# A preactivated 3x3 convolution: the sum of x taken from plane C, and the mean subtracted from C in place

## The chip, the cores and the metric

The kernel runs on one core of one Trainium2 chip. The metric is the device time of one execution in microseconds (us), the median of several runs. In the text TensorE is PE, VectorE is DVE, ScalarE is ACT, GpSimd is POOL and SyncE is SP, as in the rows.

## What is computed

The input x has 32 images of 128 channels and 56 x 56 pixels in float32. Each image is normalized in 32 groups of 4 channels, convolved with a 3 x 3 kernel whose weights take only the values Wp, 0 and -Wn, and added to x.

```python
def _quantize(weight, Wp, Wn):
    max_val = jnp.max(jnp.abs(weight))
    w_norm = weight / safe_max                       # safe_max = max_val, or 1 where that is 0
    delta = 0.05 * jnp.max(jnp.abs(w_norm))
    tern = where(w_norm > delta, 1.0, where(w_norm < -delta, -1.0, 0.0))
    return where(tern > 0, Wp[0] * tern, where(tern < 0, Wn[0] * tern, tern))

def _gn(v):                                          # groups of 4 channels, all pixels
    return ((g - mean(g)) / jnp.sqrt(var(g) + 1e-5)).reshape(v.shape)

out = x + conv3x3(_gn(x), _quantize(weight, Wp, Wn)) + bias
```

## The kernel before

**The planes.** The 128 channels lie on the partitions. The kernel pairs the image rows and forms four planes of 28 x 56 from an image: C, the sum of an even row and the odd row below it (less two means); D, odd less even; A, an odd row less the odd row before it; B, an even row less the even row after it. The 3 x 3 convolution of the two rows of a pair then needs four products of three taps, C, D, A and B, in place of six: C and A go to the even output rows, D and B to the odd ones. Each plane is scaled by 256 over the standard deviation and split into two float16 parts: hi on ScalarE (`make_hi`, line 394) and lo, the rest, on VectorE (`make_lo`, line 617). TensorE multiplies both parts with the ternary weights (`multiply`, line 786), in 24 matmuls for a product, four banks of 6. `lo X(k)` here is lo of plane X of image k.

**The statistics.** ScalarE sums x (`sum_x`, line 400, one pass over 3136 columns). A matmul with a matrix of group means turns the sum into a mean, one column in PSUM (`sum_mean`, line 772); ScalarE reads it as the negative mean and twice that (`take_mean`, lines 425 and 426). A second pass on ScalarE sums the squares of x less the mean (`sum_squares`, line 440), a second column gives the variance (`sum_var`, line 777), and VectorE and ScalarE make the scale of it (`variance`, `root`, `first_rstd`, `newton_factor`, `scale_of_x`). VectorE forms C with two means added in the same instruction (`make_c`, line 571), D (577) and A (583); GpSimd forms B (331). Only the outer row of A and of B needs the mean by itself: two short ScalarE instructions (`edges`, lines 433 and 434), which must be done before hi A and hi B.

**The slots.** Every engine runs through the same sequence of slots, written by hand: `emit(prev, now, nxt, far)` lists what the engine does while image `now` is multiplied, for the image after it (`nxt`) and the one after that (`far`). Waits are on semaphores with counts; no scheduler moves anything. In a middle slot k, TensorE does C(k), the variance of k+1, D(k), A(k), the mean of k+2, B(k). ScalarE does hi A(k), hi B(k), the root of k+1, the copy of C(k) out of PSUM (which A(k) waits for), the sum of x of k+2, the copy of D(k) (which B(k) waits for), hi C(k+1), the mean of k+2, hi D(k+1), the squares of k+2, the edges of k+1. VectorE does lo D(k), the variance of k+1, lo A(k), C, D and A of k+1 with the small steps of the scale between them, lo B(k), lo C(k+1), and four instructions that write output rows from PSUM (line 632). GpSimd does plane B of k+1 once lo C(k+1) is done, beside these four. The start has slots of its own: `first_slot` (k = -1, no product), `second_slot` (k = 0) and, on two engines, `third_slot` (k = 1).

**Data in and out.** SP loads x in halves into four buffers and stores the output; GpSimd's queue adds x to the output rows by an accumulating DMA. A buffer of x is loaded again when all planes, edges and squares of its image are done.

**The weights.** Before the first product VectorE finds the largest weight of a channel (line 525), TensorE turns the column, and `ternary_weights` (lines 530 to 540) divides the weights by the maximum and compares them; TensorE then turns them (`turn_weights`, line 751, 18 matmuls for C and D and 6 for A and B), VectorE casts them to float16 (line 561).

## Time and profile before

| | us |
|---|---|
| median of 3 runs (561.44 to 563.65) | 561.8 |
| span of the profiled execution | 559.9 |
| PE busy | 530.8 (95%) |
| DVE busy | 540.4 (97%) |
| ACT busy | 508.4 (91%) |
| POOL busy | 159.9 (29%) |

The span goes from the first to the last instruction of the one profiled execution; the rest of its time lies around it. Busy times are unions over an engine's instructions, which overlap at their ends (a start that lies up to 0.1 us ahead of the end in the row before it is no error). In the chain of work that ended last, PE has 46%, DVE 30%, time in which the engine waited for nothing that the profile shows 19%, and ACT 2%. TensorE's granted clock was 0.996 of full speed on average.

### The profile page before, as it was taken

The page shows a single profiled execution, that of the slowest core. Times are in us where ns is not written, and L with a number is a line of the kernel's source. Part 1 is how long each engine was busy: PE and PEld are TensorE (multiplying, and loading weights), DVE is VectorE, ACT ScalarE, POOL GpSimd, SP SyncE. Part 2 cuts the span into 40 slices and gives each one's busy share as a digit, 9 for nine tenths or more (in the row PEclk, how much of TensorE's full clock was granted, in tenths as well). Part 3 has the DMA queues.
Part 4 walks back from the last instruction along what each step waited for, and adds up shares of the span by engine and source line. Part 5 has one row for each costly group of instructions (what it writes and reads, how often), then busy time and mean ns, then how long its engine had stood idle before and what let it go on. Part 6 is the DMA issues. An engine that isn't in the chain of part 4 may idle for free.

```text
span 559.9 us, 9357 instructions
## 1 busy us (share of the span) xinstructions
PE 530.8 (95%) x3233; PEld 319.8 (57%) x3233; DVE 540.4 (97%) x507; ACT 508.4 (91%) x485; POOL 159.9 (29%) x105
## 2 busy tenths in 40 slices
PE   1898999999999999999999999999999999999994
PEld 0554565565656556555655655565565556556552
DVE  4998999999999999999999999999999999999995
ACT  4899999999999999999999999999999999999850
POOL 2021333312333321233332133333213333212330
PEclk9999999999999999999999999999999999999998
DMA  8539899999999999999999999999999999997765
GB/s 284 217 116 236 251 293 290 289 262 270 323 274 323 302 275 284 289 292 295 312 300 262 288 300 291 294 302 301 286 296 274 293 311 309 278 275 184 174 174 235
DMA packets 27960, 152.63 MB, mean 273 GB/s; under 512 B 3488, under 2 KB 3488, under 8 KB 27936
## 3 DMA queue, kind: packets, MB, share of 16 engines
q1 hardware_dynamic: 18576, 102.77, 48.5%
...
q14 instruction: 12, 0.10, 0.1%
...
## 4 chain that ended last, share of the span: by engine, by line
PE 46%; DVE 30%; issue 19%; ACT 2%; DMA 1%; DVEq 1%; ACTq 0%
PE odd_rows L786 23%; PE even_rows L786 22%; DVE parts L617 15%; DVE y L632 9%; DVE plane L583 1%; DMA x<-in_x_dram 1%; DVE newton L606 1%; DVE norm_scale L612 1%; ACT junk L440 1%; DVEq L158 0%; DVE neg_var L595 0%; DVE rstd L601 0%; PE odd_rows L777 0%; ACT junk L408 0%; PE odd_rows L772 0%
## 5 line engine op out<-in xcount | busy, mean ns | idle before, releaser
L786 PE MATMUL odd_rows<-parts,w_lhsT 128*128 128x385 f16 (+1 forms) x1536 | 266.1, 330 | 3.4 <-DVE parts L617 3.1
L786 PE MATMUL even_rows<-parts,w_lhsT 128*128 128x385 f16 (+1 forms) x1536 | 265.6, 330 | 2.9 <-DVE parts L617 1.9
L617 DVE SCALAR_TENSOR_TENSOR parts<-plane,norm_scale,parts 128x1568 f16<-128x1568 f32 x127 | 233.8, 1844 | 1.8 <-ACT parts L394 1.8
L331 POOL TENSOR_TENSOR plane<-x 128x1512 f32<-128x1512 f32 x31 | 105.8, 3413 | 374.3 <-DVE parts L617 374.3
L786 PEld LDWEIGHTS even_rows<-parts,w_lhsT 128*128 128x128 f16 x1536 | 150.1, 98 | 108.3 <-DVE parts L617 2.6
L394 ACT ACTIVATE parts<-plane,norm_scale 128x1568 f16<-128x1568 f32 x127 | 199.8, 1596 | 9.7 <-ACT plane L434 5.2
L786 PEld LDWEIGHTS odd_rows<-parts,w_lhsT 128*128 128x128 f16 x1536 | 147.9, 99 | 102.7 <-DVE parts L617 4.4
L440 ACT ACTIVATE junk<-x,negmean 128x3136 f16<-128x3136 f32 x32 | 92.9, 2904 | 0.1
L400 ACT ACTIVATE junk<-x 128x3136 f16<-128x3136 f32 x31 | 87.0, 2806 | 0.0
L632 DVE SCALAR_TENSOR_TENSOR y<-even_rows,out_scale,d_sb 128x784 f32<-128x784 f32 x62 | 63.7, 1027 | 0.0
L632 DVE SCALAR_TENSOR_TENSOR y<-odd_rows,out_scale,c_sb 128x784 f32<-128x784 f32 x62 | 63.6, 1026 | 0.0
L571 DVE SCALAR_TENSOR_TENSOR plane<-x,neg2mean 128x1568 f32<-128x1568 f32 x32 | 58.7, 1834 | 0.0
L577 DVE TENSOR_TENSOR plane<-x 128x1568 f32<-128x1568 f32 x32 | 57.0, 1783 | 0.6 <-ACT junk L408 0.6
L385 ACT ACTIVATE d_sb<-odd_rows,bias_sb,out_scale 128x1568 f32<-128x1568 f32 x32 | 52.7, 1647 | 5.0 <-PE odd_rows L786 5.0
L583 DVE TENSOR_TENSOR plane<-x 128x1512 f32<-128x1512 f32 x32 | 55.3, 1727 | 0.0
L379 ACT ACTIVATE c_sb<-even_rows,bias_sb,out_scale 128x1568 f32<-128x1568 f32 x32 | 53.0, 1657 | 1.2 <-PE even_rows L786 0.8
L344 POOL DMA_DIRECT2D y<-in_x_dram x61 | 52.8, 873 | 4.5 <-issue 4.5
L425 ACT ACTIVATE neg2mean<-odd_rows 128x1 f32<-128x1 f32 x32 | 5.5, 171 | 15.0 <-PE odd_rows L772 13.9
L777 PEld LDWEIGHTS odd_rows<-sums,group_mean 128*128 128x128 f32 x64 | 11.6, 194 | 5.6 <-issue 3.5
L772 PEld LDWEIGHTS odd_rows<-sums,group_mean 128*128 128x128 f32 x62 | 10.9, 190 | 4.2 <-DVE parts L617 1.8
L777 PE MATMUL odd_rows<-sums,group_mean 128*128 128x1 f32 x64 | 9.2, 213 | 3.4 <-ACT junk L440 3.4
L433 ACT ACTIVATE plane<-x,negmean 128x56 f32<-128x56 f32 x32 | 10.6, 332 | 0.0
...
## 6 DMA issues: line engine op xcount, KB each, us to landing
...
wp_sb<-in_L_conv_Wp_dram ACTq DMA_DIRECT2D x1, 0.5 KB, 7.6
wn_sb<-in_L_conv_Wn_dram ACTq DMA_DIRECT2D x1, 0.5 KB, 8.0
bias_sb<-in_L_conv_bias_dram ACTq DMA_DIRECT2D x1, 0.5 KB, 7.7
```

The lines of the kernel that those rows point to most:

```text
L331: nc.gpsimd.tensor_tensor(plane[B][:, 0:PAIRS - 1, :], even[:, 0:PAIRS - 1, :], even[:, 1:, :], ALU.subtract).then_inc(plane_ready[B], 1)
L344: pool.dma_start(y, of, accum_op=ALU.add).then_inc(residual_added[img.buf][h], 16)
L379: nc.scalar.activation(c_sb[:], product_ps(EVEN), ACT.Identity, bias=(no_bias if p else bias_sb)[:, 0:1], scale=out_scale[:, p, 0:1]).then ...
L394: nc.scalar.activation(part(img, j, HI), plane[j][:], ACT.Copy, scale=norm_scale[:, b_slice(img)]).then_inc(hi_ready[j], 1)
L400: nc.scalar.activation(junk[:], x_sb[img.buf][:].rearrange("p h w -> p (h w)"), ACT.Copy, accum_out=sums[:, img.buf, 1:2]).then_inc(sum_re ...
L440: nc.scalar.activation(junk[:], x_sb[img.buf][:].rearrange("p h w -> p (h w)"), ACT.Square, bias=negmean[:, b_slice(img)], accum_out=sums[ ...
L571: nc.vector.scalar_tensor_tensor(plane[C][:], xs[:, 0:H:2, :], neg2mean[:, b_slice(img)], xs[:, 1:H:2, :], ALU.add, ALU.add).then_inc(plan ...
L577: nc.vector.tensor_tensor(plane[D][:], xs[:, 1:H:2, :], xs[:, 0:H:2, :], ALU.subtract).then_inc(plane_ready[D], 1)
L583: nc.vector.tensor_tensor(plane[A][:, 1:, :], odd[:, 1:, :], odd[:, 0:PAIRS - 1, :], ALU.subtract).then_inc(plane_ready[A], 1)
L617: nc.vector.scalar_tensor_tensor(part(img, j, LO), plane[j][:], norm_scale[:, b_slice(img)], part(img, j, HI), ALU.mult, ALU.subtract).the ...
L632: nc.vector.scalar_tensor_tensor(rows_of(y_sb[img.buf], h, odd), product_ps(odd, 2 * h, 2 * h + 2), out_scale[:, p, 0:1], other[:, 2 * h:2 ...
L786: ins = nc.tensor.matmul(product_ps(odd, b, b + 1)[:, 0, :, to:to + n], w_lhsT[:, prod, kw, :], part(img, prod, which)[:, b * BANK_ROWS:(b ...
```

## The change

- The pass that sums x on ScalarE (`sum_x`, and `sum_first_x` in halves for image 0) is gone. VectorE forms C without the mean, with a multiplication by 1.0 in the place of the column of means, and lets the same instruction write its sum as the sum of x (`make_c`; `make_first_c` in halves). C is formed for `far`, one slot earlier than before, so there are two buffers for it (`plane[C]` and `other_c`).
- ScalarE adds the two negative means to C in place (`centre`), behind the squares of the same image and ahead of the edges.
- The weights are compared with plus and minus 0.05 of their maximum, without being divided: ten instructions become six.
- In the first slots the order changes on four engines: GpSimd forms plane B of image 0 once the ternary weights are there (VectorE did, `make_first_b`); TensorE turns the weights of C and D ahead of the first variance, and forms the mean of image 1 behind the wait for lo D(0) and its variance ahead of the last bank of D(0); VectorE forms C(1) ahead of the weight casts for A and B, and D(1) and A(1) in slot 0; ScalarE copies C(0) behind hi B(0).

```diff
-    def difference_b(img):
+    def difference_b(img, first=False):
-        pool.wait_ge(lo_ready[C], img.count(plus=1))
+        if first:
+            pool.wait_ge(w_ternary, p + 1)
+        else:
+            pool.wait_ge(lo_ready[C], img.count(plus=1))
...
-        if now and nxt:
-            difference_b(nxt)
+        if nxt:
+            difference_b(nxt, first=not now)
...
-    def sum_x(img):
-        act.wait_ge(x_loaded[img.buf], img.turn * 32 + 32)
-        wait(act, sumsq_ready, img.count())
-        nc.scalar.activation(junk[:], x_sb[img.buf][:].rearrange("p h w -> p (h w)"), ACT.Copy,
-                             accum_out=sums[:, img.buf, 1:2]).then_inc(sum_ready, 1)
-    def sum_first_x(img):
-        act.wait_ge(half_x_loaded, 16 * (p + 1))
-        wait(act, sumsq_ready, img.count())
-        halves = [x_sb[img.buf][:, 2 * ROWS * h:2 * ROWS * (h + 1), :].rearrange("p h w -> p (h w)")
-                  for h in range(HALVES)]
-        nc.scalar.activation(junk[:, 0:2 * COLS], halves[0], ACT.Copy,
-                             accum_out=first_sum[:]).then_inc(x_loaded[img.buf], 16)
-        act.wait_ge(x_loaded[img.buf], img.turn * 32 + 32)
-        nc.scalar.activation(junk[:, 2 * COLS:4 * COLS], halves[1], ACT.Copy,
-                             accum_out=sums[:, img.buf, 1:2]).then_inc(sum_ready, 1)
+    def centre(img):
+        act.wait_ge(sum_ready, img.count(plus=1))
+        act.wait_ge(negmean_ready, img.count(plus=1))
+        c = plane_of(img, C)
+        nc.scalar.activation(c[:], c[:], ACT.Identity,
+                             bias=neg2mean[:, b_slice(img)]).then_inc(plane_ready[C], 1)
...
     def emit(prev, now, nxt, far):
         first_slot, second_slot = not now and not prev, now and not prev
         if first_slot:
-            sum_first_x(nxt)
             take_mean(nxt)
             sum_squares(nxt)
+            centre(nxt)
+            root(nxt)
             edges(nxt)
-            root(nxt)
-            sum_x(far)
             make_first_hi(nxt)
             make_hi(nxt, D)
         if second_slot:
             take_mean(nxt)
             sum_squares(nxt)
             make_hi(now, A)
-            copy_c(now)
             make_hi(now, B)
             root(nxt)
+            copy_c(now)
+            centre(nxt)
             copy_d(now)
             make_hi(nxt, C)
-            sum_x(far)
         elif now:
-            third_slot = prev.j == 0 and prev.q == p * N_IMG // X_BUFS
-            if third_slot:
-                copy_c(now)
             make_hi(now, A)
             make_hi(now, B)
             if nxt:
                 root(nxt)
-            if not third_slot:
-                copy_c(now)
-            if far:
-                sum_x(far)
+            copy_c(now)
             copy_d(now)
             if nxt:
                 make_hi(nxt, C)
                 sum_squares(far)
+                centre(far)
...
 def ternary_weights():
-    step(nc.vector.tensor_scalar(col[0], w_max[:], 0.0, None, ALU.is_equal))
-    step(nc.vector.tensor_tensor(col[1], w_max[:], col[0], ALU.add))
-    step(nc.vector.reciprocal(col[2], col[1]))
-    nc.vector.tensor_scalar(w_raw, w_raw, col[2], None, ALU.mult)
-    step(nc.vector.tensor_scalar(col[3], w_max[:], col[2], THRESHOLD, ALU.mult, ALU.mult))
-    step(nc.vector.tensor_scalar(col[4], col[3], -1.0, None, ALU.mult))
+    nc.vector.tensor_scalar(above[:], w_max[:], THRESHOLD, None, ALU.mult)
+    nc.vector.tensor_scalar(below[:], w_max[:], -THRESHOLD, None, ALU.mult).then_inc(w_step, 1)
+    steps[0] += 1
-    step(nc.vector.tensor_scalar(neg, w_raw, col[4], equal[:], ALU.is_lt, ALU.mult))
-    nc.vector.scalar_tensor_tensor(pos, w_raw, col[3], neg, ALU.is_gt, ALU.subtract).then_inc(w_ternary, 1)
+    step(nc.vector.tensor_scalar(neg, w_raw, below[:], equal[:], ALU.is_lt, ALU.mult))
+    nc.vector.scalar_tensor_tensor(pos, w_raw, above[:], neg, ALU.is_gt, ALU.subtract).then_inc(w_ternary, 1)
-    nc.vector.tensor_scalar(neg, w_raw, col[2], col[4], ALU.mult, ALU.is_lt).then_inc(w_ternary, 1)
+    nc.vector.tensor_scalar(neg, w_raw, below[:], None, ALU.is_lt).then_inc(w_ternary, 1)
...
     def make_c(img):
-        dve.wait_ge(negmean_ready, img.count(plus=1))
-        plane_free(img, C)
+        dve.wait_ge(x_loaded[img.buf], img.turn * 32 + 32)
+        wait(dve, lo_ready[C], img.count(plus=-1))
-        nc.vector.scalar_tensor_tensor(plane[C][:], xs[:, 0:H:2, :], neg2mean[:, b_slice(img)],
-                                       xs[:, 1:H:2, :], ALU.add, ALU.add).then_inc(plane_ready[C], 1)
+        nc.vector.scalar_tensor_tensor(plane_of(img, C)[:], xs[:, 0:H:2, :], 1.0, xs[:, 1:H:2, :], ALU.mult, ALU.add,
+                                       accum_out=sums[:, img.buf, 1:2]).then_inc(sum_ready, 1)
+    def make_first_c(img, h):
+        if h == 0:
+            dve.wait_ge(half_x_loaded, 16 * (p + 1))
+            wait(dve, lo_ready[C], img.count(plus=-1))
+        else:
+            dve.wait_ge(x_loaded[img.buf], img.turn * 32 + 32)
+        xs, rows = x_sb[img.buf], slice(h * ROWS, (h + 1) * ROWS)
+        ins = nc.vector.scalar_tensor_tensor(plane_of(img, C)[:, rows], xs[:, 0:H:2, :][:, rows], 1.0, xs[:, 1:H:2, :][:, rows],
+                                             ALU.mult, ALU.add,
+                                             accum_out=sums[:, img.buf, 1:2] if h else first_sum[:])
+        if h == 0:
+            ins.then_inc(x_loaded[img.buf], 16)
+        else:
+            ins.then_inc(sum_ready, 1)
...
-    def make_first_b(img):
-        plane_free(img, B)
...
         if first_slot:
             if p == 0:
                 local_max()
-            make_d(nxt)
+            make_first_c(nxt, 0)
+            make_first_c(nxt, 1)
             if p == 0:
                 ternary_weights()
+            make_d(nxt)
             variance(nxt)
-            make_c(nxt)
+            turned_weights((C, D))
             first_rstd(nxt)
             newton_factor(nxt)
             scale_of_x(nxt)
-            turned_weights((C, D))
             make_first_lo(nxt)
         if second_slot:
+            make_c(nxt)
             turned_weights((A, B))
             make_lo(now, D)
             make_a(now)
-            make_first_b(now)
-            variance(nxt)
             if p == 0:
                 output_scales()
+            variance(nxt)
             make_lo(now, A)
-            make_c(nxt)
+            make_lo(now, B)
+            make_d(nxt)
             first_rstd(nxt)
+            make_a(nxt)
             newton_factor(nxt)
             scale_of_x(nxt)
-            make_lo(now, B)
-            make_d(nxt)
+            make_c(far)
             make_lo(nxt, C)
         elif now:
-            third_slot = prev.j == 0 and prev.q == p * N_IMG // X_BUFS
             make_lo(now, D)
-            if third_slot:
-                make_a(now)
             if nxt:
                 variance(nxt)
             make_lo(now, A)
             if nxt:
                 first_rstd(nxt)
-                make_c(nxt)
+            if far:
+                make_c(far)
+            if nxt:
                 newton_factor(nxt)
                 make_d(nxt)
                 scale_of_x(nxt)
...
                 turn_max()
             sum_first_mean(nxt)
             pe.wait_ge(negmean_ready, nxt.count(plus=1))
+            turn_weights((C, D))
             sum_var(nxt, start=True)
-            turn_weights()
+            turn_weights((A, B))
             warm_up()
             pe.wait_ge(var_ready, nxt.count(plus=1))
-            sum_mean(far, start=True)
         if second_slot:
             pe.wait_ge(w_ready, 4 * p + 2)
         if now:
...
                 sum_var(nxt, start=True)
             pe.wait_ge(lo_ready[D], now.count(plus=1))
             if second_slot:
+                sum_mean(nxt, start=True)
+            multiply(now, D, 0)
+            if second_slot:
                 pe.wait_ge(w_ready, 4 * p + 4)
-            multiply(now, D, 0)
             multiply(now, D, 1)
+            multiply(now, D, 2)
             if second_slot:
                 pe.wait_ge(negmean_ready, nxt.count(plus=1))
-                sum_var(nxt, start=True)
-            multiply(now, D, 2)
+                sum_var(nxt, start=False)
             if nxt:
                 pe.wait_ge(var_ready, nxt.count(plus=1))
             multiply(now, D, 3)
```

ScalarE in a middle slot, before: from the mean of image 4 (buffer x0) to the copy of C, with `plane1` D, `plane2` A, `plane3` B and `plane0` C.

```order
L425 ACTIVATE neg2mean<-odd_rows 128x1
L426 ACTIVATE negmean<-odd_rows 128x1
L394 ACTIVATE parts<-plane1,norm_scale 128x1568
L440 ACTIVATE junk,sums<-x0,negmean 128x3136
L433 ACTIVATE plane2<-x3,negmean 128x56
L434 ACTIVATE plane3<-x3,negmean 128x56
L394 ACTIVATE parts<-plane2,norm_scale 128x1568
L394 ACTIVATE parts<-plane3,norm_scale 128x1568
L446 ACTIVATE std<-neg_var 128x1
L379 ACTIVATE c_sb<-even_rows,bias_sb,out_scale 128x1568
L400 ACTIVATE junk,sums<-x1 128x3136
```

And in the changed kernel, the same stretch:

```order
L424 ACTIVATE neg2mean<-odd_rows 128x1
L425 ACTIVATE negmean<-odd_rows 128x1
L402 ACTIVATE parts<-plane1,norm_scale 128x1568
L438 ACTIVATE junk,sums<-x0,negmean 128x3136
L410 ACTIVATE plane0<-plane0,neg2mean 128x1568
L432 ACTIVATE plane2<-x3,negmean 128x56
L433 ACTIVATE plane3<-x3,negmean 128x56
L402 ACTIVATE parts<-plane2,norm_scale 128x1568
L402 ACTIVATE parts<-plane3,norm_scale 128x1568
L444 ACTIVATE std<-neg_var 128x1
L387 ACTIVATE c_sb<-even_rows,bias_sb,out_scale 128x1568
```

The centring of C stands between the squares and the two edge rows, and the sum of x is gone from behind the copy of C.

ScalarE in slot 0, before: from the mean of image 1 to the copy of D(0).

```order
L425 ACTIVATE neg2mean<-odd_rows 128x1
L426 ACTIVATE negmean<-odd_rows 128x1
L440 ACTIVATE junk,sums<-x1,negmean 128x3136
L394 ACTIVATE parts<-plane2,norm_scale 128x1568
L379 ACTIVATE c_sb<-even_rows,bias_sb,out_scale 128x1568
L394 ACTIVATE parts<-plane3,norm_scale 128x1568
L446 ACTIVATE std<-neg_var 128x1
L385 ACTIVATE d_sb<-odd_rows,bias_sb,out_scale 128x1568
```

And in the changed kernel:

```order
L424 ACTIVATE neg2mean<-odd_rows 128x1
L425 ACTIVATE negmean<-odd_rows 128x1
L438 ACTIVATE junk,sums<-x1,negmean 128x3136
L402 ACTIVATE parts<-plane2,norm_scale 128x1568
L402 ACTIVATE parts<-plane3,norm_scale 128x1568
L444 ACTIVATE std<-neg_var 128x1
L387 ACTIVATE c_sb<-even_rows,bias_sb,out_scale 128x1568
L410 ACTIVATE other_c<-other_c,neg2mean 128x1568
L393 ACTIVATE d_sb<-odd_rows,bias_sb,out_scale 128x1568
```

The copy of C(0) moved behind hi B(0) and the root, and the centring of C(1) came in ahead of the copy of D(0).

TensorE from the weights' turning to the first bank of C(0), before (line 772 is the mean of image 1):

```order
L777 MATMUL odd_rows<-sums,group_mean 128x1
L751 MATMUL even_rows<-turn,w_pos 128x128 x18
L751 MATMUL odd_rows<-turn,w_pos 128x128 x6
L760 MATMUL odd_rows<-turn 128x384 x6
L772 MATMUL odd_rows<-sums,group_mean 128x1
L786 MATMUL even_rows<-parts,w_lhsT 128x392
```

And in the changed kernel, from the weights to the first matmul of C(0) (line 776 is the first variance):

```order
L750 MATMUL even_rows<-turn,w_pos 128x128 x18
L776 MATMUL odd_rows<-sums,group_mean 128x1
L750 MATMUL odd_rows<-turn,w_pos 128x128 x6
L759 MATMUL odd_rows<-turn 128x384 x6
L785 MATMUL even_rows<-parts,w_lhsT 128x392
```

Further on in the changed kernel, the last matmuls of C(0), and the first of D(0) (line 771 is the mean of image 1):

```order
L785 MATMUL even_rows<-parts,w_lhsT 128x392 x2
L785 MATMUL even_rows<-parts,w_lhsT 128x7x55 x4
L785 MATMUL even_rows<-parts,w_lhsT 128x392
L771 MATMUL odd_rows<-sums,group_mean 128x1
L785 MATMUL odd_rows<-parts,w_lhsT 128x392
```

The mean of image 1 moved from ahead of C(0) to the place between C(0) and D(0), and the first variance behind 18 weight matmuls.

## Rows read from the trace of the kernel before

**Rows 1.** Windows: stretch, length, busy time of PE, PEld, DVE, ACT, POOL, then PEclk, DMA, GB/s.
```profile
260.96:326.78 65.82, 65.45 (x401) 39.49 (x401) 65.60 (x62) 63.29 (x61) 20.30 (x12) 1.00 1.02 295
```

**Rows 2.** Timeline of slot 16: start, length, engine, line, operation, out<-in, count, idle before.
```profile
293.86 4.16 PE L786 MATMUL odd_rows<-parts,w_lhsT 128*128 128x392 f16 x24 [0.18 <-DVE parts L617]
...
301.85 0.28 PE L772 MATMUL odd_rows<-sums,group_mean 128*128 128x1 f32 x2
...
302.16 0.17 ACT L425 ACTIVATE neg2mean<-odd_rows 128x1 f32<-128x1 f32 x1 [0.54 <-PE odd_rows L772]
...
302.28 1.60 ACT L394 ACTIVATE parts<-plane,norm_scale 128x1568 f16<-128x1568 f32 x1
...
307.40 3.10 ACT L394 ACTIVATE parts<-plane,norm_scale 128x1568 f16<-128x1568 f32 x2 [0.17 <-ACT plane L434]
...
309.96 0.28 PE L777 MATMUL odd_rows<-sums,group_mean 128*128 128x1 f32 x2
...
310.22 4.16 PE L786 MATMUL odd_rows<-parts,w_lhsT 128*128 128x392 f16 x24
310.27 0.16 DVE L595 TENSOR_SCALAR neg_var<-odd_rows 128x1 f32<-128x1 f32 x1
310.35 1.85 DVE L617 SCALAR_TENSOR_TENSOR parts<-plane,norm_scale,parts 128x1568 f16<-128x1568 f32 x1
...
323.84 3.10 ACT L394 ACTIVATE parts<-plane,norm_scale 128x1568 f16<-128x1568 f32 x2 [0.17 <-ACT plane L434]
...
326.78 1.50 PE L786 MATMUL odd_rows<-parts,w_lhsT 128*128 128x392 f16 x8 [0.18 <-DVE parts L617]
```

**Rows 3.** Groups of DVE and ACT from 62 to 522.41: count | busy, mean ns.
```profile
L571 DVE SCALAR_TENSOR_TENSOR plane<-x,neg2mean 128x1568 f32<-128x1568 f32 x28 | 51.3, 1833 | 0.0
L577 DVE TENSOR_TENSOR plane<-x 128x1568 f32<-128x1568 f32 x28 | 49.9, 1782 | 0.0
...
L394 ACT ACTIVATE parts<-plane,norm_scale 128x1568 f16<-128x1568 f32 x112 | 176.3, 1596 | 5.0 <-ACT plane L434 4.9
...
L400 ACT ACTIVATE junk<-x 128x3136 f16<-128x3136 f32 x28 | 78.6, 2806 | 0.0
...
L400 ACT ACTIVATION_READ_ACCUMULATOR junk<-x 128x1 f32 x28 | 5.3, 190 | 0.0
```

**Rows 4.** Timeline of the start, columns as in rows 2.
```profile
7.58 1.35 DVE L525 TENSOR_REDUCE w_absmax<-y 128x1 f32<-128x1152 f32 x1 [6.51 <-DMA y<-in_L_conv_weight_dram]
...
14.44 1.42 DVE L540 SCALAR_TENSOR_TENSOR w_pos<-y,w_consts,w_neg 128x1152 f16<-128x1152 f32 x1
...
20.25 0.28 PE L772 MATMUL odd_rows<-sums,group_mean 128*128 128x1 f32 x2
...
21.52 4.15 PE L786 MATMUL even_rows<-parts,w_lhsT 128*128 128x392 f16 x24 [0.99 <-DVE parts L623]
...
22.78 2.91 ACT L440 ACTIVATE junk<-x,negmean 128x3136 f16<-128x3136 f32 x1
...
25.50 2.16 PE L786 MATMUL odd_rows<-parts,w_lhsT 128*128 128x392 f16 x12
...
28.59 1.83 DVE L617 SCALAR_TENSOR_TENSOR parts<-plane,norm_scale,parts 128x1568 f16<-128x1568 f32 x1
...
30.50 4.15 PE L786 MATMUL even_rows<-parts,w_lhsT 128*128 128x392 f16 x24 [0.71 <-DVE parts L617]
...
47.06 1.85 DVE L617 SCALAR_TENSOR_TENSOR parts<-plane,norm_scale,parts 128x1568 f16<-128x1568 f32 x1 [1.77 <-ACT parts L394]
```

**Rows 5.** The chain that ended last, in order of time: start, length, what.
```profile
63.49 4.16 PE odd_rows L786 x24
```

**Rows 6.** Groups of the whole span, shapes apart: count | busy, mean ns | idle before.
```profile
L331 POOL TENSOR_TENSOR plane<-x 128x1512 f32<-128x1512 f32 x31 | 105.8, 3413 | 374.3 <-DVE parts L617 374.3
...
L623 DVE SCALAR_TENSOR_TENSOR parts<-plane,norm_scale,parts 128x784 f16<-128x784 f32 x2 | 2.0, 1031 | 0.6 <-ACT parts L419 0.6
```

**Rows 7.** Windows at the end, columns as in rows 1.
```profile
552.80:554.00 1.20, 0.01 (x1) 0.00 (x0) 0.63 (x1) 0.00 (x0) 0.00 (x0) 1.00 0.81 319
...
555.00:556.00 1.00, 0.00 (x0) 0.00 (x0) 0.00 (x0) 0.00 (x0) 0.00 (x0) 0.92 1.00 392
```

23 lines of the change are left out of this document (11 added, 12 removed).

## The prediction

> Times are microseconds from the start of the profiled span. Slot k is the time in which TensorE forms the four products C(k), D(k), A(k), B(k) of image k; hi and lo are the two float16 parts that ScalarE and VectorE make of each plane.
>
> **What bounds the kernel now.** I read the stretches first. In 65.82 us of the middle TensorE is busy for 65.45, VectorE for 65.60 and ScalarE for 63.29 [rows 1]: two engines are full and a third nearly so, and all matter there. Which wait ends last is then read from the timeline of one slot [rows 2], where the reader should follow two paths that leave D(16) at 293.86.
>
> The first path bounds it. After D and A, TensorE runs B(16) and C(17), then the column that sums the squares of image 18 (309.96). VectorE takes it up at 310.27 and starts lo A(17) at 310.35, 16.49 after D(16). From there VectorE works through a whole slot without a pause to lo D(18), and D(18) starts at 326.78, 16.43 later [rows 2]. The loop covers two slots and costs 32.92, so 16.46 each.
>
> The second path has room. It leaves TensorE's mean column of image 18 at 301.85; ScalarE then does hi D(17) from 302.28, the squares of image 18, the two edge rows, and hi A(17) from 307.40 [rows 2]. One hi lasts 1.60 [rows 3], so hi A(17) is there at 309.00, and lo A(17) could not start before 310.35. The spare time is 1.35.
>
> In the start, the waits are elsewhere: lo A(1) starts at 47.06 after 1.77 idle us, and its releaser is hi on ScalarE [rows 4]. The chain that ended last then has D(2) at 63.49 [rows 5], 16.43 behind lo A(1), that is one slot of VectorE's work.
>
> **Steady slots: the pass that sums x goes, a pass that centres C comes.** ScalarE loses a pass of 2.81 with its read of 0.19 and gains one of the form of hi, 1.60, of which 0.10 overlaps (two hi take 3.10) [rows 2, 3]. It has 1.4 us less work per slot. But the work changes place. The pass that goes stood between the copies of C and D, ahead of the mean; ScalarE waited for the mean anyway (0.54 idle in front of 302.16, a wait that now grows). The pass that comes stands behind the squares and ahead of the edge rows and hi A, on the second path, which starts at the mean and cannot start earlier. So hi A(17) moves by 1.50 to 308.90 and ends at 310.50, and lo A(17) starts 16.64 to 16.66 after D(16), where it was 16.49. In slot 17 the same sum from 310.22 and 323.84 gives 16.72 to 16.74. I take 16.70: the 1.35 that covered the path is used up, and 0.21 is left over per loop. Behind the waiting lo A stand all of VectorE's later instructions and so D(18).
>
> VectorE's own pass for C changes form: an immediate in place of the column of means, and a sum beside it. The nearest row for the first is the two-input pass without a column, 1782 against 1833 ns [rows 3], a gain of 0.05 at most. No row of VectorE shows a pass with a sum. ScalarE's reads of its sum last 190 ns [rows 3]; behind a small VectorE instruction the next one starts after 0.08 (310.27 to 310.35) [rows 2]. So the read costs between 0 and 0.19, and I take 0.08, VectorE's own row. Together the pass changes by +0.03, with ends of -0.05 and +0.19. It reads x of image k+2 at the place in the slot where the sum read it, so no load is needed earlier, and the buffer that a load fills is freed by planes that were finished two slots before.
>
> The loop becomes 16.70 + 16.43 + 0.03 = 33.16, against 32.92 before: +0.12 per slot. From D(2) to D(30) there are 28 slots: **+3.4**, with ends of +2.2 and +5.6. Here the gain in ScalarE's work goes into its wait for the mean.
>
> **The start.** The weight comparison loses three small steps and a pass over the weights. The maximum of the weights ends at 8.93 as before [rows 4]. Two half passes for C(0) follow, 1.03 each by the half-size row [rows 6], to 11.0; then six instructions instead of ten, and the ternary weights end near 14.0 where they end at 15.86 now. That brings the first product from 21.52 to about 20.6 [rows 4]. What follows gives it back, in this order.
>
> 1. C(1) is now formed (1.84) between lo C(0) and the weight casts, so lo D(0) ends at 25.9 and D(0) starts at about 26.2 instead of 25.50.
> 2. The mean of image 1 moves in TensorE's queue from 20.25, ahead of C(0), to behind the wait for lo D(0): 26.2 less the 0.3 of its own time. ScalarE's squares of image 1 start at 26.4 instead of 22.78 [rows 4]. They last 2.9 and stand ahead of hi A(0), which starts at 29.3; lo A(0) starts at 30.9 instead of 28.59.
> 3. The copy of C moves behind hi B(0) and the root: 32.4 to 34.1. A(0) needs it, and starts at 34.1 instead of 30.50 [rows 4].
> 4. The mean of image 2 follows the third bank of B(0): 34.1 + 4.0 + 3.0 = 41.1. From a mean to hi D is 0.43 [rows 2], then hi D(1) 41.6, squares 43.1, centring 46.0, edges 47.5, hi A(1) 48.2, lo A(1) 49.9. Before it was 47.06.
>
> So D(2) comes **2.8** later. The first plane B goes from VectorE (1.73) to GpSimd, beside other work; its saving is in VectorE's idle time in these slots, not on this chain. Since the chain holds one pass with a sum, and one variance column that queues behind 18 weight turns, I give it 2.3 to 3.5.
>
> **The end.** Slot 30 has no image 32, so the pass for C falls out of VectorE's slot and TensorE can run its four products of 4.0 back to back: 16.0 against 16.46, **-0.5**.
>
> **The sum.** +3.4 + 2.8 - 0.5 = +5.7. The profiled span is 559.9, so 565.6 for the new span. The median of the runs is 561.8, 1.9 above the span, and I carry that over: **567.5**, with 565.8 to 570.4 from the ends.
>
> **Two rules weighed against the rows.** The pass for C, with two float32 inputs in SBUF, takes 1833 ns, and the plain two-input pass of the same size 1782 [rows 3]: reading two such inputs does not halve this instruction. The Trainium skill (Vector Engine (DVE) Microarchitecture Reference, 7. Points that are easy to get wrong) says that this instruction with two sources in SBUF that are not bf16 has half the throughput, with no port left for reading back the accumulator. The trace disagrees for the form without a sum, and no run here shows the form with one.
> GpSimd's pass for plane B runs only beside VectorE's output rows, and has waited 374.3 us in all for lo C to let it [rows 6]. After the change its first one starts with the ternary weights at 14.0, beside VectorE's D(0). The Trainium skill (SBUF — State Buffer, Who interferes with whom) says that a VectorE instruction with two SBUF inputs contends with a GpSimd instruction that reads SBUF, and that whichever issues first blocks the other for its whole length. No run here shows it.
>
> **The rivals.**
> - *The pass with a sum runs at half rate.* A column costs (1844 - 1031) / 784 = 1.04 ns [rows 3, 6], so 1568 more cost 1.63 on VectorE per slot. VectorE alone then sets the slot at about 18.0: 28 x 1.5 + 2.8 + 2, about 609. For it: the form is new. Against: the same form without a sum is at full rate. Chance 0.04.
> - *GpSimd gets ahead in the start.* D(0)'s pass then starts at 17.4 instead of 13.9, and with its slack ahead of the variance the chain slips by about 2.5: 570.0. Against: VectorE's pass stands directly behind the weights on its own queue, GpSimd waits for a semaphore; and if VectorE is first, GpSimd is done at 15.7 + 3.4 = 19.1, before lo C(0) at 19.5. Chance 0.08.
> - *TensorE's clock falls in slot 0.* It now stands idle from the end of D(0), about 31.0, to 34.1. After the last product the clock stayed at 2.4 GHz through 552.8 to 555 and fell to 1.2 within the next microsecond, its mean 0.92 [rows 7]: 3.1 us of idle time is just short of that. If it falls, A(0) takes up to 8.0 instead of 4.0; I take half of that, +2: 569.5. Chance 0.10.
> - *The second path does not end last.* If hi A comes 0.2 earlier than I add up, the slots stay at 16.46: 561.8 + 2.8 - 0.5 = 564.1, about no change. Chance 0.14.
> - *Faster.* The start is set by VectorE's work and not by ScalarE's: 1.9 of weights and 1.7 of plane B go, and 1.8 of C(2) comes earlier, so D(2) is 1.8 earlier; and ScalarE's spare time lets VectorE and TensorE run at 16.36 a slot, as between D(16) and D(17), where TensorE waits for nothing [rows 2], -2.8: 561.8 - 1.8 - 2.8 - 0.5 = 556.7. It decides from whether the mean reaches ScalarE before hi D is due. Against: the mean's place in TensorE's queue is fixed behind A. Chance 0.08.
>
> **How the numbers follow.** The forecast has 0.56. A measurement of this kernel can tell about 0.5% from no change, 2.8 us, so slower begins at 564.6. Slower is the forecast with the first three rivals, 0.78; same is the fourth, 0.14; faster is the fifth, 0.08. The range from 564.0 to 570.5 holds all but the first and the last rival, 0.88; without the fourth it would hold 0.74, too little.
>
> **What would show it.** Right: lo A waits for hi A on ScalarE in the middle slots, each slot 16.5 to 16.6; D(2) near 66.3, A(0) near 34 behind the copy of C; the last full slot 16.0; the pass with its read at 1.8 to 2.0. Wrong: D(2) before 64, lo A without a wait, a pass for C of 3.4, or a clock below 1 before 60.

## The result, and the profile after

| | before | after |
|---|---|---|
| median, us (lowest to highest of 4 runs) | 562.04 (561.44 to 563.65) | 568.5 (567.66 to 569.35) |
| span of the profiled execution, us | 559.9 | 567.7 |
| mean granted clock in it | 0.996 | 0.989 |

The ratio is 1.0115, with an interval of 1.0101 to 1.0129: slower by a little over 1%, as forecast, and 1.0 us above the 567.5 that was predicted. The four executions of the changed kernel are not alike: spans of 567.7 and 567.6 at clocks of 0.989 and 0.992, and twice 566.0 at 0.995. The profiled one is the slowest; its own time is 569.35, 1.65 above its span, and 1.6 to 1.75 is what lies around the span in all runs here.

The page of the kernel after, busy time and share of each engine (first line) and the granted clock in 40 slices:

```profile
PE 535.5 (94%) x3233; PEld 319.4 (56%) x3233; DVE 537.8 (95%) x536; ACT 466.0 (82%) x451; POOL 164.9 (29%) x106
...
PEclk9979899999999999999999999999999999999999
```

ScalarE lost 42 us of work (508.4 before) and the kernel got slower. The second line shows where to look first: the clock has a 7 in the third slice (28.4 to 42.6 us) and an 8 in the fifth (56.8 to 71); before, the first 39 slices are all at 9:

```profile
PEclk9999999999999999999999999999999999999998
```

The chain of work that ended last, after (start, length, what; columns as in [rows 5]):

```profile
33.96 6.96 PE even_rows L785 x24
55.61 5.82 PE even_rows L785 x24
...
284.69 4.16 PE odd_rows L785 x24
...
317.75 4.16 PE odd_rows L785 x24
...
516.08 4.16 PE odd_rows L785 x24
```

The first two rows are A(0) and A(1): the same 24 products that take 4.15 elsewhere take 6.96 and 5.82 here. The rest are D(15), D(17) and D(29), and D(17) is 33.06 behind D(15): that is the loop of two slots that the prediction speaks of, 33.16 in its sum and 32.92 before [rows 2]. It runs over the odd slots here, over the even ones before.

The timeline of slot 15 after, from D(15) at 284.69 on (columns as in [rows 2]):

```profile
292.67 0.28 PE L771 MATMUL odd_rows<-sums,group_mean 128*128 128x1 f32 x2
...
294.60 2.91 ACT L438 ACTIVATE junk<-x,negmean 128x3136 f16<-128x3136 f32 x1
...
297.49 1.59 ACT L410 ACTIVATE other_c<-other_c,neg2mean 128x1568 f32<-128x1568 f32 x1
...
299.74 3.10 ACT L402 ACTIVATE parts<-plane,norm_scale 128x1568 f16<-128x1568 f32 x2 [0.19 <-ACT plane L433]
...
301.10 0.16 DVE L593 TENSOR_SCALAR neg_var<-odd_rows 128x1 f32<-128x1 f32 x1 [0.15 <-PE odd_rows L776]
...
301.37 1.85 DVE L615 SCALAR_TENSOR_TENSOR parts<-plane,norm_scale,parts 128x1568 f16<-128x1568 f32 x1
...
303.21 1.77 DVE L560 SCALAR_TENSOR_TENSOR plane<-x 128x1568 f32<-128x1568 f32 x1
...
304.91 0.08 DVE L560 DVE_READ_ACCUMULATOR plane<-x 128x1 f32 x1
304.91 0.27 DVE L604 TENSOR_SCALAR newton<-rstd,neg_var 128x1 f32<-128x1 f32 x1
...
317.75 4.16 PE L785 MATMUL odd_rows<-parts,w_lhsT 128*128 128x392 f16 x24 [0.31 <-DVE parts L615]
```

Read it from the mean column (292.67) to the squares (294.60), the centring pass (297.49), hi A (299.74 to 301.34) and lo A (301.37). The variance, which ended last before, is done by 301.26: lo A(16) now follows hi A(16), 16.68 behind D(15). The last row, D(17), shows the other half of the loop, 317.75 - 301.37 = 16.38.

The timeline of the start after:

```profile
13.87 4.82 POOL L339 TENSOR_TENSOR plane<-x 128x1512 f32<-128x1512 f32 x1 [10.17 <-DVE w_pos L528]
...
20.25 4.15 PE L785 MATMUL even_rows<-parts,w_lhsT 128*128 128x392 f16 x24 [1.36 <-DVE parts L621]
...
26.19 2.91 ACT L438 ACTIVATE junk<-x,negmean 128x3136 f16<-128x3136 f32 x1
...
32.17 1.64 ACT L387 ACTIVATE c_sb<-even_rows,bias_sb,out_scale 128x1568 f32<-128x1568 f32 x1
...
33.96 6.96 PE L785 MATMUL even_rows<-parts,w_lhsT 128*128 128x392 f16 x24 [2.85 <-ACT c_sb L387]
...
43.74 0.28 PE L771 MATMUL odd_rows<-sums,group_mean 128*128 128x1 f32 x2
...
52.37 1.85 DVE L615 SCALAR_TENSOR_TENSOR parts<-plane,norm_scale,parts 128x1568 f16<-128x1568 f32 x1 [2.55 <-ACT parts L402]
...
55.61 5.82 PE L785 MATMUL even_rows<-parts,w_lhsT 128*128 128x392 f16 x24 [1.98 <-ACT c_sb L387]
```

Up to the start of A(0) every step lies within 0.5 of the list in the prediction. Then A(0), behind 2.85 us without work, takes 2.8 too long, and the mean of image 2 (43.74), lo A(1) (52.37) and D(2) (69.52) are late with it. The windows over these stretches (columns as in [rows 1]) have TensorE's granted clock as the third number from the end: 0.61 of 2.4 GHz is a mean over both levels, for the most part at the lower one, 1.2.

```profile
31.00:35.00 4.00, 1.16 (x5) 0.54 (x5) 4.00 (x3) 4.00 (x4) 0.00 (x0) 0.74 0.44 180
35.00:41.00 6.00, 6.00 (x24) 2.86 (x23) 5.96 (x8) 3.45 (x3) 0.00 (x0) 0.61 0.00 0
...
56.00:62.00 6.00, 6.00 (x29) 3.25 (x28) 6.00 (x6) 3.03 (x5) 0.00 (x0) 0.72 1.01 396
```

The fall need not lie in the gap itself. Ahead of A(0) it does (0.94 in the microsecond from 32, 0.50 in the next one). A(1) starts at 55.61, and its clock falls only in the microsecond from 56:

```profile
55.00:56.00 1.00, 0.39 (x3) 0.28 (x4) 1.00 (x3) 1.00 (x2) 0.00 (x0) 1.00 0.99 295
56.00:57.00 1.00, 1.00 (x7) 0.56 (x6) 1.00 (x2) 1.00 (x1) 0.00 (x0) 0.89 1.02 427
57.00:58.00 1.00, 1.00 (x4) 0.45 (x3) 1.00 (x3) 0.01 (x1) 0.00 (x0) 0.50 1.00 410
```

Set against the terms of the sum, in the two profiled executions (D(30) starts at 524.23 before and at 532.38 after):

| term | predicted | measured |
|---|---|---|
| D(2) | +2.8 | 63.49 to 69.52: +6.0 |
| 28 slots | +3.4 | 16.455 to 16.531 each: +2.1 |
| D(30) to D(31) | -0.5 | 16.46 to 15.96: -0.5 |
| behind D(31) | 0 | 19.21 to 19.36: +0.15 |
| span | +5.7 | +7.8 |

The sum was 2.1 short of the profiled span and 1.0 short of the median, and two of its terms were off in opposite directions. The experiments ask for the cause of each.

### The profile page after: what moved, and what is told of

The parts are those of the page before. It is cut to its first block, busy times and chain, and to the rows that moved or that the text cites. A ratio compares the mean times of both kernels' runs of the same rounds, so it can differ in the third digit from the quotient of the medians.

```text
span 567.7 us, 9307 instructions
## 1 busy us (share of the span) xinstructions
PE 535.5 (94%) x3233; PEld 319.4 (56%) x3233; DVE 537.8 (95%) x536; ACT 466.0 (82%) x451; POOL 164.9 (29%) x106
## 4 chain that ended last, share of the span: by engine, by line
PE 30%; DVE 28%; ACT 19%; issue 19%; DMA 1%; DVEq 1%; ACTq 0%
DVE parts L615 16%; PE even_rows L785 15%; PE odd_rows L785 14%; DVE y L630 8%; ACT junk L438 8%; ACT parts L402 5%; ACT other_c L410 4%; DMA y<-in_L_conv_weight_dram 1%; ACT plane L433 1%; ACT plane L432 1%; DVE norm_scale L610 1%; ACT c_sb L387 1%; DVE newton L604 1%; DVEq L160 0%; DVE plane L560 0%
## 5 line engine op out<-in xcount | busy, mean ns | idle before, releaser
L785 PE MATMUL even_rows<-parts,w_lhsT 128*128 128x385 f16 (+1 forms) x1536 | 270.2, 333 | 6.2 <-ACT c_sb L387 4.8
L339 POOL TENSOR_TENSOR plane<-x 128x1512 f32<-128x1512 f32 x32 | 110.7, 3459 | 375.4 <-DVE parts L615 365.2
L615 DVE SCALAR_TENSOR_TENSOR parts<-plane,norm_scale,parts 128x1568 f16<-128x1568 f32 x111 | 204.1, 1842 | 5.0 <-ACT parts L402 3.4
L402 ACT ACTIVATE parts<-plane,norm_scale 128x1568 f16<-128x1568 f32 x111 | 174.3, 1596 | 8.5 <-ACT plane L433 5.2
L615 DVE SCALAR_TENSOR_TENSOR parts<-other_c,norm_scale,parts 128x1568 f16<-128x1568 f32 x16 | 29.5, 1843 | 0.0
L402 ACT ACTIVATE parts<-other_c,norm_scale 128x1568 f16<-128x1568 f32 x16 | 25.6, 1602 | 3.9 <-DVE norm_scale L610 3.9
L560 DVE SCALAR_TENSOR_TENSOR other_c<-x 128x1568 f32<-128x1568 f32 x16 | 28.3, 1771 | 0.0
L560 DVE SCALAR_TENSOR_TENSOR plane<-x 128x1568 f32<-128x1568 f32 x15 | 26.6, 1772 | 0.0
L410 ACT ACTIVATE plane<-plane,neg2mean 128x1568 f32<-128x1568 f32 x16 | 25.5, 1596 | 0.0
L410 ACT ACTIVATE other_c<-other_c,neg2mean 128x1568 f32<-128x1568 f32 x16 | 25.5, 1595 | 0.0
```

Source lines behind the costliest of these rows:

```text
L339: nc.gpsimd.tensor_tensor(plane[B][:, 0:PAIRS - 1, :], even[:, 0:PAIRS - 1, :], even[:, 1:, :], ALU.subtract).then_inc(plane_ready[B], 1)
L402: nc.scalar.activation(part(img, j, HI), plane_of(img, j)[:], ACT.Copy, scale=norm_scale[:, b_slice(img)]).then_inc(hi_ready[j], 1)
L410: nc.scalar.activation(c[:], c[:], ACT.Identity, bias=neg2mean[:, b_slice(img)]).then_inc(plane_ready[C], 1)
L560: nc.vector.scalar_tensor_tensor(plane_of(img, C)[:], xs[:, 0:H:2, :], 1.0, xs[:, 1:H:2, :], ALU.mult, ALU.add, accum_out=sums[:, img.buf, ...
L615: nc.vector.scalar_tensor_tensor(part(img, j, LO), plane_of(img, j)[:], norm_scale[:, b_slice(img)], part(img, j, HI), ALU.mult, ALU.subtr ...
L785: ins = nc.tensor.matmul(product_ps(odd, b, b + 1)[:, 0, :, to:to + n], w_lhsT[:, prod, kw, :], part(img, prod, which)[:, b * BANK_ROWS:(b ...
```

## Experiments

Each run stands beside runs of the kernel before on the same chip, and ratios are to those. Their medians lie between 561.6 and 562.0, so a time that is set against the changed kernel's 568.5 is good to about 0.4. A slot is (D(30) - D(2)) / 28 from the trace of the run.

### Is it the centring pass that sets the slot?

```diff
                         copy_c(now)
+                        if nxt:
+                            centre(nxt)
                         copy_d(now)
...
                             sum_squares(far)
-                            centre(far)
```

> The changed kernel with one pass moved: from slot 1 on ScalarE centres plane C of image k+1 between its copies of C and D in slot k, where the pass that sums x stood, instead of centring image k+2 behind the squares and ahead of the edge rows and hi A. Theory (the second path, mean to hi A to lo A, sets the 16.53 of a slot because the centring pass of 1.6 stands on it): hi A comes 1.5 earlier, lo A waits for the variance column and not for hi A, a slot is 16.43 or less, D(2) is 1.5 earlier too since the centring of image 2 leaves slot 0; together -1.5 - 28 x 0.10 = -4.3, a span near 563.4. Rival (VectorE's own work or its new order sets the slot, the pass with the sum included): the slot stays at 16.53 and only the 1.5 of the start goes, a span near 566.2.

Measured: 562.82, ratio 1.0032 (1.0018 to 1.0046), span 560.5. From the timeline of this run, D(2) and D(30):

```profile
65.42 4.16 PE L786 MATMUL odd_rows<-parts,w_lhsT 128*128 128x392 f16 x24 [0.23 <-DVE parts L616]
...
525.45 4.16 PE L786 MATMUL odd_rows<-parts,w_lhsT 128*128 128x392 f16 x24 [0.19 <-DVE parts L616]
```

The slot is (525.45 - 65.42) / 28 = 16.430, as the theory had it, and 28 x 0.101 = 2.8 us are back with VectorE's work unchanged. So the place of the centring pass set the slot, not the pass with the sum and not VectorE's order. The span is 2.9 shorter than expected, and that is the start: D(2) is 4.1 earlier and not 1.5, because TensorE's gap ahead of A(1) shrank to 0.49 and A(1) took 4.15 again, and because A(0), behind the same 2.85 of waiting, took 5.51 and not 6.96, its clock still fallen but for a shorter time.

### Is it the clock that made A(0) and A(1) slow?

TensorE forms the last bank of D(0) three times and that of D(1) twice; the extra ones keep it busy where it would wait.

```diff
+                        for _ in range(2 if second_slot else 1 if prev and prev.j == 0 else 0):
+                            multiply(now, D, 3, again=True)
                         multiply(now, D, 3)
```

> The changed kernel, with TensorE's last bank of D(0) formed three times instead of once and that of D(1) twice (each overwrites the one before; 1.0 us each), so that it stands idle for some 0.9 us ahead of A(0) and A(1) instead of 2.85 and 1.98. Theory (the granted clock fell in these two gaps, and A(0) and A(1) were slow for that): the clock stays at 1.00, A(0) still starts near 33.96 but lasts 4.15 instead of 6.96, the mean of image 2 comes 2.8 earlier, A(1) lasts 4.15 instead of 5.82, D(2) is 2.8 to 4.5 earlier than 69.52; a span of 563.2 to 564.9. Rival (the two products were slow because of something else, such as what ScalarE and VectorE do beside them): A(0) stays near 7.0 and the time the same, 567.7, or up to 1 later by the extra banks.

Measured: 565.4, ratio 1.0066 (1.0049 to 1.0083), span 563.8. The second of the three windows above, in this run:

```profile
35.00:41.00 6.00, 6.00 (x39) 3.67 (x36) 5.96 (x8) 3.35 (x3) 0.00 (x0) 1.00 0.00 0
```

A(0) and D(2) in its timeline:

```profile
33.85 4.15 PE L785 MATMUL even_rows<-parts,w_lhsT 128*128 128x392 f16 x24 [0.85 <-ACT c_sb L387]
...
65.83 4.16 PE L785 MATMUL odd_rows<-parts,w_lhsT 128*128 128x392 f16 x24 [0.23 <-DVE parts L615]
```

A(0) starts where it did and takes 4.15 at a clock of 1.00; so does A(1). D(2) is 3.7 earlier, the slot stays at 16.52. With more work for TensorE the kernel is 3.9 shorter in the span and 3.1 in the median. All four executions lie between 565.0 and 565.5, where those of the changed kernel spread over 1.7. What is left of the start in this run is 65.83 - 63.49 = +2.3, against the predicted +2.8.

### Does the late mean cost the rest of the start?

```diff
                         multiply(now, C, 2)
+                        if second_slot:
+                            sum_mean(nxt, start=True)
                         multiply(now, C, 3)
...
                         pe.wait_ge(lo_ready[D], now.count(plus=1))
-                        if second_slot:
-                            sum_mean(nxt, start=True)
                         multiply(now, D, 0)
```

> The changed kernel, with the mean column of image 1 put back in front of the last bank of C(0) on TensorE, instead of behind the wait for lo D(0). Theory (the start lost most by this move: squares of image 1 at 26.19 instead of 22.78, ahead of hi A(0) on ScalarE): the squares start near 23.6, hi A(0) near 27.6 instead of 29.09, A(0) near 32.4 instead of 33.96, and TensorE's gap ahead of it is 1.3 instead of 2.85; if the clock holds, D(2) is 1.6 + 2.8 earlier and with the second fall gone up to 6.1: a span of 561.6 to 563.3. Rival (VectorE sets hi A(0) by its plane A, and the gaps stay over 2): A(0) within 0.5 of 33.96, a span of 567 or more.

Measured: 565.58, ratio 1.0059 (1.0037 to 1.008), span 565.8. The first 18 products of C(0), and A(0), in its timeline:

```profile
19.99 4.83 PE L785 MATMUL even_rows<-parts,w_lhsT 128*128 128x392 f16 x18 [2.19 <-DVE parts L621]
...
33.00 5.83 PE L785 MATMUL even_rows<-parts,w_lhsT 128*128 128x392 f16 x24 [2.52 <-ACT c_sb L387]
```

The start missed what was expected, and so did its rival: A(0) came 1.0 earlier, not 1.6, since in this execution the clock fell already in C(0) (0.61 in the microsecond from 20; 18 products take 3.15 at full clock) and put the mean at 24.65, where it comes at 23.30 in the run with all three places mended below; it fell again in A(0) and A(1). D(2) came at 67.44. So a part of the start is shown to hang on the mean, 1.0 at A(0), and how much more without the falls this run can't say. Its four executions are the longer, the lower their clock: 567.46, 566.05, 565.11 and 563.46 us at mean clocks of 0.988, 0.991, 0.995 and 0.997.

### Does an earlier copy of C help?

```diff
                         make_hi(now, A)
+                        copy_c(now)
                         make_hi(now, B)
                         root(nxt)
-                        copy_c(now)
                         centre(nxt)
```

(and the same in slot 1)

> The changed kernel, with the copy of C of images 0 and 1 ahead of hi B on ScalarE in slots 0 and 1, instead of behind it and the root. Theory (A(0) waits for that copy, and the wait is long enough for the clock to fall): A(0) starts near 32.5 instead of 33.96 behind a gap of 1.3, keeps the clock and ends before 37, so that the mean of image 2 comes some 4 earlier; hi B and all behind it on VectorE come 1.6 later, which gives back some 1.7 by D(2): D(2) near 67, a span of 564.5 to 566. Rival (what A(0) and D(2) wait for is not the copy): A(0) stays near 34 and D(2) near 69.5, or later by the 1.6, a span of 567.7 to 569.3.

Measured: 568.63, ratio 1.0123 (1.0107 to 1.014), span 567.0: nothing gained. A(0), and the late mean of image 3 and B(1) behind it, in the timeline:

```profile
32.55 5.59 PE L789 MATMUL even_rows<-parts,w_lhsT 128*128 128x392 f16 x24 [1.51 <-DVE parts L619]
...
58.71 0.38 PE L775 MATMUL odd_rows<-sums,group_mean 128*128 128x1 f32 x2 [2.09 <-DVE parts L619]
...
58.95 5.83 PE L789 MATMUL odd_rows<-parts,w_lhsT 128*128 128x392 f16 x24
```

The theory was half right. A(0) came at 32.55, so it did wait for the copy; but its clock fell all the same, behind a gap of 1.51. And hi B, now behind the copy, moved the gap to B(1), which waited 2.09 for lo B(1) and then ran 5.83. D(2) came at 68.74, 0.8 earlier than in the changed kernel. The exchange closes no gap, it moves one from A(1) to B(1); alone it gains nothing.

### What does the weight comparison alone bring?

```diff
-                step(nc.vector.tensor_scalar(col[0], w_max[:], 0.0, None, ALU.is_equal))
-                step(nc.vector.tensor_tensor(col[1], w_max[:], col[0], ALU.add))
-                step(nc.vector.reciprocal(col[2], col[1]))
-                nc.vector.tensor_scalar(w_raw, w_raw, col[2], None, ALU.mult)
...
+                nc.vector.tensor_scalar(col[3], w_max[:], THRESHOLD, None, ALU.mult)
+                step(nc.vector.tensor_scalar(col[4], w_max[:], -THRESHOLD, None, ALU.mult))
```

> The kernel before, with the weight comparison of the changed kernel alone (six instructions on VectorE instead of ten), all else as it was. Theory (ScalarE's sum of image 1 stands ahead of hi C(0), which therefore starts at 19.38 whatever the weights do): the ternary weights are done near 14.0 instead of 15.86, the first product stays near 21.5 and D(2) near 63.5, time within 0.5 of the kernel before. Rival (the weights set the first product): the first product near 19.7 and the time 1.8 shorter.

Measured: 561.98, ratio 1.0005 (0.9994 to 1.0015). The weights and the first product in its timeline:

```profile
12.79 1.42 DVE L536 SCALAR_TENSOR_TENSOR w_pos<-y,w_consts,w_neg 128x1152 f16<-128x1152 f32 x1
...
21.37 4.15 PE L782 MATMUL even_rows<-parts,w_lhsT 128*128 128x392 f16 x24 [1.53 <-DVE parts L619]
```

The weights are ready 1.65 earlier (14.21 against 15.86) and the first product 0.15 (21.37 against 21.52 [rows 4]); even that is not theirs, as ScalarE's squares of image 0, which do not wait for them, start 0.15 earlier too (12.38 against 12.53). In the kernel before, this work is covered by ScalarE's sum of image 1, which holds hi C(0) back to 19.2. Only where that sum is gone, as in the changed kernel, do the weights move the first product (20.25); the run after the next one, in which they end 2.74 later and the first product starts 2.74 later, shows it.

### What does the sum in the pass for C cost?

```diff
-                                                   xs[:, 1:H:2, :], ALU.add, ALU.add).then_inc(plane_ready[C], 1)
+                                                   xs[:, 1:H:2, :], ALU.add, ALU.add,
+                                                   accum_out=spare_sum[:]).then_inc(plane_ready[C], 1)
```

> The kernel before with one thing of the change alone: VectorE's pass for plane C also sums what it writes, into a column that nothing reads; the column of means stays its operand, and ScalarE's own pass that sums x stays. Theory (VectorE's read of its sum lies beside the next instruction and costs nothing, and the 0.05 that the pass is shorter in the changed kernel is the immediate in place of the column): the pass stays at 1.83, the next instruction starts 1.75 to 1.76 behind it as before, the slot stays at 16.46, the time within 0.5. Rival (the sum is paid for in part): 0.08 more in each of 31 passes, of which every second lies on the loop, 1.2 longer; with 0.19 it would be 2.9.

Measured: 562.11, ratio 1.0003 (0.999 to 1.0017), slot 16.46. Three rows in the middle of its timeline:

```profile
295.82 1.83 DVE L572 SCALAR_TENSOR_TENSOR plane<-x,neg2mean 128x1568 f32<-128x1568 f32 x1
297.58 0.08 DVE L572 DVE_READ_ACCUMULATOR plane<-x,neg2mean 128x1 f32 x1
297.58 0.27 DVE L608 TENSOR_SCALAR newton<-rstd,neg_var 128x1 f32<-128x1 f32 x1
```

The read of 0.08 starts together with the next instruction and costs nothing. In the changed kernel the next instruction comes 1.70 behind the pass (303.21 to 304.91 above), here 1.76: what is left to make it shorter there is the immediate, with a multiplication in place of an addition. The two were not tried apart.

### Do GpSimd and VectorE keep each other out?

```diff
-                    if first:
-                        pool.wait_ge(w_ternary, p + 1)
-                    else:
+                    if not first:
                         pool.wait_ge(lo_ready[C], img.count(plus=1))
```

> The changed kernel, with GpSimd's first plane B waiting for the image alone and no longer for the ternary weights, so that it starts near 10 and runs beside VectorE's second half pass for C(0) and the weights. Theory (two-input passes of the two engines exclude each other, whichever is first keeps the other out): GpSimd's pass starts behind the half pass and lasts 3.4, and VectorE's last weight instruction, with two inputs, waits for its end: w_pos ends up to 1 later than 13.72. Rival (they only share): both run side by side, GpSimd's pass near 4 and VectorE's instructions at their old lengths; w_pos ends at 13.7.

One execution, 570.35, span 568.7. GpSimd's plane B and a small VectorE instruction in its timeline:

```profile
9.89 4.17 POOL L337 TENSOR_TENSOR plane<-x 128x1512 f32<-128x1512 f32 x1 [6.20 <-DVE plane L568]
...
11.20 2.89 DVE L524 TENSOR_TENSOR equal<-wp_sb,wn_sb 128x1 f32<-128x1 f32 x1
```

The theory holds, at another instruction than it named: the comparison of wp and wn, one element in each partition, is VectorE's first with two inputs in SBUF; it takes 0.15 in the changed kernel and 2.89 here, and ends at 14.09, as GpSimd's pass does (14.06). All of VectorE's queue stands behind it: w_pos ends at 16.46 instead of 13.72, not within 1 of it. The first product moves from 20.25 to 22.99. In the changed kernel the pass runs the other way round: VectorE's D(0) starts at 13.64, GpSimd's pass at 13.87, and it takes 4.82 instead of 3.41, beside nothing that waits for it. The Trainium skill (SBUF — State Buffer, Who interferes with whom) has it that the two engines share a pair of ports, and that whichever takes it first blocks the other for its whole instruction. Here that is seen in both directions.

### Mending all three places

```diff
-WARM_UP = 6
+WARM_UP = 9
...
+                        if second_slot:
+                            multiply(now, D, 3, again=True)
                         multiply(now, D, 3)
```

together with the edits of the first and the third experiment above.

> The changed kernel with the three places mended at once: image k+1's plane C centred between the copies of C and D in slot k (as in the run with the centring pass moved), the mean column of image 1 ahead of the last bank of C(0), and TensorE kept busy in its gaps by nine warm-up products instead of six and by forming the last bank of D(0) twice. Theory (three separate losses: the second path in the slots, the late mean and the fallen clock in the start): no fall of the clock ahead of 70, A(0) near 32.5 with 4.15, D(2) 2.5 to 3.5 earlier than the 65.42 of the run with the centring pass moved, so 62 to 63; the slot 16.43; a span of 557 to 558, that is 2 to 3 shorter than the kernel before. Rival (the gains share one wait, so that the start stays near 65): a span of 559.5 to 561.

Measured: 559.83, ratio 0.9965 (0.9951 to 0.9979), span 558.1: 0.35% shorter than the kernel before, clear of the interval. D(2) is at 62.62, D(30) at 522.69, the slot 16.431, A(0) at 32.12 and 4.15 long, and the windows from 18 to 70 all have a clock of 1.00. D(2) lies in the range of the theory of three separate losses, the span 0.1 above it. The edits came together, so the run does not say how much of the start each of them gave back.

### What is the room on ScalarE worth?

On top of that, ScalarE forms Newton's factor and the scale of x, and VectorE no longer does:

```diff
+                def scale_by_scalar(img):
+                    b = b_slice(img)
+                    act.wait_ge(rstd_ready, img.count(plus=1))
+                    nc.scalar.activation(square[:, b], rstd0[:, b], ACT.Square).then_inc(square_ready, 1)
...
+                    nc.scalar.activation(newton[:, b], square[:, b], ACT.Identity, bias=three[:, 0:1],
+                                         scale=neg_var[:, b]).then_inc(newton_ready, 1)
...
+                    nc.scalar.activation(norm_scale[:, b], rstd0[:, b], ACT.Copy,
+                                         scale=newton[:, b]).then_inc(scale_of_x_ready, 1)
```

> The kernel of the run with the three places mended, and in the slots from 1 on the two small steps behind the reciprocal (Newton's factor and the scale of x) formed by three small ScalarE instructions between its centring of C and its copy of D, instead of by two on VectorE (0.19 and 0.12 from start to start). Theory (with the second path out of the way VectorE's row of work sets the slot, 16.43 against the 16.36 in which TensorE waits for nothing, as between D(16) and D(17) of the kernel before): VectorE's 0.31 leave the loop until TensorE is the bound, the slot falls to 16.36 to 16.39, 1.2 to 2.0 shorter in all, a span of 556.1 to 557. Rival (ScalarE's longer row delays hi C or the copies, and they set the slot): the slot stays at 16.43 or grows, a span of 558 or more.

Measured: 555.33, ratio 0.989 (0.9873 to 0.9906), span 553.7. A window in the middle:

```profile
260.00:326.00 66.00, 66.00 (x407) 39.91 (x406) 65.25 (x58) 62.02 (x70) 20.35 (x12) 1.00 1.01 294
```

D(2) and D(30) in its timeline:

```profile
62.59 4.16 PE L800 MATMUL odd_rows<-parts,w_lhsT 128*128 128x392 f16 x24 [0.23 <-DVE parts L632]
...
518.42 4.16 PE L800 MATMUL odd_rows<-parts,w_lhsT 128*128 128x392 f16 x24
```

The slot is 16.280, below the expected 16.36 to 16.39: slot 16 of the kernel before, from which that floor was read, is one slot only, and held D(17) back to 0.26 behind its variance column [rows 2], where 0.14 is to be seen in half the slots here. TensorE is now busy for all 66.00 us of the window and has 89% of the chain that ended last (46% in the kernel before): it is the bound. The same edit on the kernel before:

> The kernel before, with the same two steps moved from VectorE to ScalarE as in the run of the fastest kernel (Newton's factor and the scale of x, in the slots from 1 on, here between ScalarE's sum of x and its copy of D). Theory (it is the room on ScalarE, made by taking the sum of x off it, that this move lives on): ScalarE works 15.82 us of each 16.46 in the kernel before and the three instructions take 0.85 more with their waits, so that its row needs 16.7 to 16.85 and sets the slot; 28 slots at +0.25 to +0.4, a span of 567 to 571. Rival (the waits for the mean leave enough room, and VectorE's relief pays here as well): a slot of 16.28 to 16.40, a span of 555 to 558.

Measured: 563.86, ratio 1.0034 (1.0022 to 1.0046). Two hi A of ScalarE, one slot apart, in the timeline:

```profile
292.22 3.10 ACT L397 ACTIVATE parts<-plane,norm_scale 128x1568 f16<-128x1568 f32 x2 [0.20 <-ACT plane L437]
...
308.76 3.10 ACT L397 ACTIVATE parts<-plane,norm_scale 128x1568 f16<-128x1568 f32 x2 [0.17 <-ACT plane L437]
```

The window in the middle:

```profile
260.00:326.00 66.00, 65.31 (x401) 39.37 (x399) 64.43 (x53) 65.03 (x73) 20.14 (x13) 1.00 1.02 293
```

There ScalarE is busy for 65.03 of 66, its row of work takes 16.54 without a wait for another engine, and the slot grows to 16.525. The sign is the theory's; its size, 0.25 to 0.4, was too large, as it added up busy times that overlap at their ends. So the same two steps cost 0.07 per slot where ScalarE still sums x, and bring 0.15 where it does not: the room that the change makes on ScalarE is real, but it pays only once something is moved into it and the new pass stands off the path.

## Why the prediction came out, and where its steps were off

**The steady slots.** The mechanism was right: the centring pass of 1.5 stands on the path from the mean to hi A, uses up its 1.35, and lo A follows hi A. lo A starts 16.68 behind D of the slot before, where 16.64 to 16.74 was forecast, and taking the pass off that path gives back all of it (first experiment). The term was mis-sized, +2.1 and not +3.4, in VectorE's half of the loop. I took +0.03 for the pass for C; it is -0.05, the lower end of the range, since the read of the sum starts beside the next instruction and the pass itself is 0.05 shorter (16.38 against 16.43). A loop of 16.70 + 16.38 = 33.08 would have been within 0.02 of the 33.06 measured, and 28 x 0.08 = +2.2.

**Half rate.** It did not come: the pass with two float32 inputs and a sum takes 1.77, the one without a sum 1.83 [rows 3]. For this form, the trace disagrees with the half throughput that the Trainium skill (Vector Engine (DVE) Microarchitecture Reference, 7. Points that are easy to get wrong) gives it.

**The start.** The order of events was right up to A(0) at 33.96 (34.1 forecast), and so was the list of what is late next, with the first product at 20.25 (20.6) and the mean of image 2 behind B(0). The step that failed is the judgement on the clock. I read from the end of the kernel that 3.1 us of idle time is just short of a fall [rows 7] and gave the fall in slot 0 a chance of 0.10 and a price of 2. It fell at both A(0) and A(1), behind 2.85 and 1.98 of waiting, and with TensorE kept busy instead D(2) comes 3.7 earlier and the median is 3.1 lower. A(0) took 2.8 longer, for which I had 2, and the second fall, 1.7 in A(1), was in no term. In the run without the falls D(2) was +2.3, close under my +2.8. The row was misread, too: the last product ends at 552.81, and a mean of 0.92 puts the fall at 555.84, 3.03 behind it, so that 3.1 was not short of it. And the end of the kernel was a poor place to read this from: what stands ahead of the gaps in the start is a TensorE with pauses, not one that has been full for 500 us. Whether that is why the clock fell sooner here was not tried. A clock below 1 before 60 was one of my signs of being wrong, and it came.

**GpSimd first.** The reason against that rival held: VectorE's pass stood ahead. Its price was not tested. The run that put GpSimd first delays the first product by 2.74, near my 2.5, but it holds up the comparison ahead of the weights and not the pass for D(0). **Second path not last** and **faster** needed hi A to be early or the mean to be off TensorE's row; neither was so. The *faster* rival's slot of 16.36 was within reach all the same: with the centring pass moved and 0.31 of VectorE's steps on ScalarE the slot is 16.28.

**The total.** 567.5 against 568.5 is closer than its steps, and that is in part luck: 1.3 too much in the slots stand against 3.2 too little in the start of the profiled execution, which is also the slowest of the four. The 1.9 from span to median was too much as well: around one span lie 1.6 to 1.75, and the rest is the spread of the runs before. The range held the time since it already reached past the clock's rival.
